# A graph-attention and mixture-of-experts layer: the node projection takes x transposed from the host, with W centred on chip

## What is computed

```python
x = x + gnn(layernorm(x), src, dst, W, b_w, a, b_a)
x = x + moe(layernorm(x), Wg, bg, W1, b1, W2, b2)

def gnn(nodes, ...):
    h = nodes @ W + b_w                      # 2500 x 512 by 512 x 512
    s_dst = h @ a[:512]; s_src = h @ a[512:]
    w = exp(leaky_relu(s_dst[dst] + s_src[src] + b_a, 0.2))
    alpha = w / segment_sum(w, dst)[dst]
    return segment_sum(alpha[:, None] * h[src], dst)
```

## Time and profile before

| | us |
|---|---|
| median of 3 runs (lowest to highest) | 864.01 (863.16 to 866.09) |
| the profiled execution, its own time | 861.91 |
| its span in the trace | 860.2 |
| busy in the span: PE, DVE, ACT, POOL | 635.0, 465.4, 370.7, 449.6 |
| mean granted TensorE clock | 0.909 of 2.4 GHz |
| first gather starts | 92.98 |

### The profile page before, as it was taken

One profiled execution on the slowest core, in us unless ns is written; L12 is line 12 of the kernel. 1 busy time (PEld: TensorE's weight loads), 2 busy tenths in 40 slices (PEclk: granted clock), 3 DMA queues, 4 the chain that ended last, 5 costly groups with the idle time before them and its releaser, 6 DMA issues.

```text
span 860.2 us, 13772 instructions
## 1 busy us (share of the span) xinstructions
PE 635.0 (74%) x2956; PEld 501.5 (58%) x2957; DVE 465.4 (54%) x1165; ACT 370.7 (43%) x982; POOL 449.6 (52%) x533
## 2 busy tenths in 40 slices
PE   4999254766776666776676676958889999999960
PEld 3777243655555555665555565745547788888840
DVE  5998433555555555565555555789495433333320
ACT  4443332434433343444343443527763454545430
POOL 5000575666666666666666666410105677777750
PEclk9999777999899998889998998887998999999995
DMA  6243475666666666666666665507994477777767
GB/s 198 100 158 106 145 214 160 180 175 177 185 175 175 178 185 175 178 182 177 177 193 169 176 192 168 146 24 263 322 376 167 90 135 136 137 132 139 134 90 249
DMA packets 58300, 146.97 MB, mean 171 GB/s; under 512 B 8868, under 2 KB 18708, under 8 KB 57880
## 3 DMA queue, kind: packets, MB, share of 16 engines
q0 software_dynamic: 35216, 106.84, 49.3%
q1 hardware_dynamic: 22968, 37.16, 12.4%
q10 hardware_dynamic: 80, 2.56, 0.9%
HBM read 118.17 MB, written 33.47 MB: 176 GB/s over the span
## 4 chain that ended last, share of the span: by engine, by line
PE 37%; DVE 22%; issue 15%; another core or an unknown queue 9%; DVEq 7%; DMA 4%; POOLq 1%; ACT 1%; POOL 1%; SPq 0%; ACTq 0%
PE ps L711 17%; PE ps L850 6%; PE ps L864 4%; DVE S L1239 4%; DVE acc L1248 4%; DVE Wt L1227 3%; PE ps L665 3%; DMA result<-y,si 2%; PE ps L840 2%; DVEq L1279 1%; PE ps L791 1%; DVEq L1248 1%; PE ps L761 1%; DMA xg<-xn_table,gi 1%
## 5 line engine op out<-in xcount | busy, mean ns | idle before, releaser
L711 PE MATMUL ps<-rows,S 128*128 128x257 f32 x1252 | 322.4, 420 | 157.6 <-DVE acc L1248 124.6
L512 POOL DMA_INDIRECT rows<-node_table,srcT x313 | 296.2, 946 | 243.4 <-issue 84.1
L711 PEld LDWEIGHTS ps<-rows,S 128*128 128x128 f32 x1252 | 260.2, 212 | 219.6 <-issue 159.2
L958 ACT ACTIVATE E<-sdst_w,rows 128x128 f32 x313 | 100.1, 390 | 281.6 <-DVE Wt L1227 150.3
L1248 DVE TENSOR_TENSOR acc<-acc,ps 64x514 f32 x160 | 110.1, 688 | 155.2 <-remote 94.5
L1239 DVE SCALAR_TENSOR_TENSOR S<-ps,lane,Wt 128x128 f32<-128x128 f32 x313 | 88.2, 345 | 22.3 <-issue 14.1
L958 ACT ACTIVATE ps<-sdst_w,rows 128x128 f32 x313 | 96.0, 351 | 0.0
L850 PE MATMUL ps<-W_e,xgT 128*128 x352 | 83.4, 380 | 0.0
L608 POOL DMA_INDIRECT result<-y,si x44 | 70.4, 1601 | 11.3 <-issue 5.8
L850 PEld LDWEIGHTS ps<-W_e,xgT 128*128 128x128 f32 x352 | 63.4, 190 | 6.9
L665 PE MATMUL ps<-Wb,xT 128*128 128x512 f32 x240 | 59.1, 403 | 2.5 <-DVE dstT L1191 1.4
(11 more groups left out here) (209 smaller groups left out, 641.9 us busy)
## 6 DMA issues: line engine op xcount, KB each, us to landing
W_e<-in_L_ffn_W_dram SPq DMA_DIRECT2D x16, 512.0 KB, 9.2
node_table<-rows SPq DMA_DIRECT2D x20, 258.0 KB, 2.6
result<-acc SPq DMA_DIRECT2D x20, 256.0 KB, 2.5
xn_table<-xn SPq DMA_DIRECT2D x20, 256.0 KB, 2.2
rows<-node_table,srcT POOLq DMA_INDIRECT x313
x_all<-in_x_dram SPq DMA_DIRECT2D x19, 256.0 KB, 3.0
out_dram<-result SPq DMA_DIRECT2D x1, 2500.0 KB, 16.7
out_dram<-result ACTq DMA_DIRECT2D x1, 2500.0 KB, 18.4
```

Of the source, the lines that this page charges most:

```text
L512: nc.gpsimd.indirect_dma_start(out=rows[:, g % RING, c, :], out_offset=None, in_=table, in_offset=bass.IndirectOffsetOnAxis(ap=srcT[:, GC ...
L711: m = pe.matmul(ps_agg[q][:, a, 0:HALF], S[:, w, c, :], rows[:, r, c, a * HALF:(a + 1) * HALF], start=(c == 0), stop=(c == n - 1))
L958: m = nc.scalar.activation(e[:, c, :], sdst_w[:, bass.ds(w, 1), :].rearrange("p w n -> p (w n)"), ACT.Exp, bias=bias, scale=scale)
```

## The change

- The host also hands over `x_cols`, x transposed in blocks: for each pair, 128 features by 4 times 256 nodes. SP loads it into `xf` (512 KB a pair) beside x itself, which is still needed for the statistics and the residual. All transposes of x on PE are gone.
- x is not normalized ahead of the product. Layernorm's mean is taken out through W: PE multiplies W by a matrix of 1/512, DVE subtracts the column means from W in place (L1124), ACT makes its high part and DVE its low part, in four pieces each. 1/std is applied behind the product, in the instruction that adds the bias (L1108).
- The high part of the transposed x is ACT's copy from SBUF (L874, both halves in one instruction). The low part is POOL's subtraction (L503), and POOL fills `acc` in ten pieces between those.
- The source and target indices come laid out by the host, and with them a copy of the targets by groups of 512, so that the smallest and largest target of a group are one reduction each.
- `load_ahead(u)` waits for the low part of pair u - 2 and its statistics. ACT's order in a step becomes `high_xT(u + 2)`, `std_of(u + 2)`, `scores(u - 1)`; DVE's `rstd_of(u)`, `normal(u + 2)`, `node_rows(u)`.

The core of the diff:

```diff
+            def load_xT(u, s):
+                sp.dma_start(xf[:, s, :, :].rearrange("p k n -> p (k n)"),
+                             x_cols[bass.ds(u, 1)].rearrange("u p c -> (u p) c")).then_inc(ld_xT[s], 16)
+            sp.dma_start(Wf[:, :, :], gnn_W.rearrange("(k p) n -> p k n", p=P)).then_inc(ld_W, 16)
+            load_xT(0, 0)
             load_x(0, 0, 0)
             load_x(0, 0, 1)
-            sp.dma_start(Wf[:, :, :], gnn_W.rearrange("(k p) n -> p k n", p=P)).then_inc(ld_W, 16)
+            load_xT(1, 1)
...
             def load_ahead(u, s, last=False):
-                for j in range(2):
-                    sp.wait_ge(xn_ok, 2 * (u - 2) + j + 1)
+                sp.wait_ge(xT_lo, u - 1)
+                load_xT(u, s)
+                sp.wait_ge(stats_ok, u - 1)
+                for j in range(2):
                     load_x(*((None, s, j) if last and j == 1 else (u, s, j)))
...
-            nc.gpsimd.memset(acc[:, :, :, :], 0.0).then_inc(ids_ok, 1)
+            for u in range(NT // 2):
+                pool.wait_ge(xT_hi, u + 1)
+                nc.gpsimd.tensor_tensor(xT[:, u % 2, 1, ...], xf[:, u % 2, ...], xT[:, u % 2, 0, ...], ALU.subtract)\
+                    .then_inc(xT_lo, 1)
+                m = nc.gpsimd.memset(acc[:, 2 * u:(2 * u + 2 if u < NT // 2 - 1 else NT + 1), :, :], 0.0)
+            m.then_inc(ids_ok, 1)
...
+            pe.wait_ge(mean_w_ok, 1)
+            pe.wait_ge(ld_W, 16)
+            for k in range(KT):
+                m = pe.matmul(ps_mean[:, :], mean_w[:, :], Wf[:, k, :], start=(k == 0), stop=(k == KT - 1))
+            m.then_inc(mean_ps, 1)
             pe.wait_ge(W_ok, 1)
             products(0, 0, True)
-            pe.wait_ge(edges_f, 1)
-            edge_columns(0)
-            edge_columns(1)
-            transposes(2, 0)
-            pe.wait_ge(edges_ok, 2)
             products(1, 1, True)
...
             def high_xT(u, s):
-                act.wait_ge(xT_ps, u + 1)
+                act.wait_ge(ld_xT[s], 16 * (u // 2) + 16 if isinstance(u, int) else u * 8 + 16 - 8 * s)
                 if not (isinstance(u, int) and u < 2):
                     act.wait_ge(h_ps, 2 * u - 2)
...
             def step(u, s, i, ahead):
-                high_xT(u + 1, 1 - s)
+                if ahead > 1:
+                    high_xT(u + 2, s)
+                    std_of(u + 2, s)
                 if not (isinstance(u, int) and u < 1):
                     scores(u - 1, 1 - s, i)
-                if ahead > 1:
-                    std_of(u + 2, s)
-                    normal(u + 2, s)
...
-                    nc.vector.tensor_tensor(halves(rows[:, s, j, 0:2 * HALF])[:, :, 0:HD], halves(ps_h[s][j]),
-                                            halves(bw_b[:, :]), ALU.add).then_inc(row_ok, 1)
+                    if j == 0:
+                        dve.wait_ge(rstd_ok, u + 1)
+                    nc.vector.scalar_tensor_tensor(out=halves(rows[:, s, j, 0:2 * HALF])[:, :, 0:HD], in0=halves(ps_h[s][j]),
+                                                   scalar=rstd[:, s, j:j + 1], in1=halves(bw_b[:, :]),
+                                                   op0=ALU.mult, op1=ALU.add).then_inc(row_ok, 1)
```

More of the change, by code:

```diff
@@ L28, in gnn_moe_kernel @@
     CH = -(-E // P)
-    CJ = -(-CH // P)
     GC = 4
@@ L637, in _ @@
             regs = [pe.alloc_register(f"pe_window{k}") for k in range(RING)]
[L638 to L646, removed]
-                for j in range(2):
-                    pe.wait_ge(xn_ok, 2 * u + j + 1)
-                    for k in range(KT):
-                        m = pe.transpose(psT[s][k // 2][:, (k % 2) * 2 * P + j * P:(k % 2) * 2 * P + (j + 1) * P],
-                                         xn[:, s, j, k * P:(k + 1) * P], ident[:, :])
-                m.then_inc(xT_ps, 1)
             def products(u, s, first):
@@ L887, in high_xT @@
             def high_xT(u, s):
-                act.wait_ge(xT_ps, u + 1)
+                act.wait_ge(ld_xT[s], 16 * (u // 2) + 16 if isinstance(u, int) else u * 8 + 16 - 8 * s)
                 if not (isinstance(u, int) and u < 2):
                     act.wait_ge(h_ps, 2 * u - 2)
-                for b in range(2):
-                    m = nc.scalar.activation(xT[:, s, 0, 2 * b:2 * b + 2, :].rearrange("p k n -> p (k n)"),
-                                             psT[s][b][:, :], ACT.Copy)
-                m.then_inc(xT_hi, 1)
-            def normal(u, s):
-                for j in range(2):
-                    act.wait_ge(rstd_ok, 4 * u + 4)
-                    if not (isinstance(u, int) and u < 2):
-                        act.wait_ge(xT_ps, u - 1)
-                    nc.scalar.activation(xn[:, s, j, :], x_of(2 * u + j), ACT.Identity, bias=shift[:, s, j:j + 1],
-                                         scale=rstd[:, s, j:j + 1]).then_inc(xn_ok, 1)
+                nc.scalar.activation(xT[:, s, 0, :, :].rearrange("p k n -> p (k n)"),
+                                     xf[:, s, :, :].rearrange("p k n -> p (k n)"), ACT.Copy).then_inc(xT_hi, 1)
+            high_xT(0, 0)
             std_of(0, 0)
-            normal(0, 0)
-            act.wait_ge(ld_W, 16)
-            nc.scalar.activation(Wb[:, 0, :, :], Wf[:, :, :], ACT.Copy).then_inc(W_hi, 1)
+            for k in range(KT):
+                act.wait_ge(Wc_ok, k + 1)
+                nc.scalar.activation(Wb[:, 0, k, :], Wf[:, k, :], ACT.Copy).then_inc(W_hi, 1)
+            high_xT(1, 1)
             std_of(1, 1)
-            normal(1, 1)
-            high_xT(0, 0)
             def scores(u, s, i):
@@ L1565 @@
     arrays, args = {}, []
+    laid = {name: _np.asarray(a) for name, a in inputs.items()}
+    n, d = laid["x"].shape
+    edges = laid["src"].shape[0]
+    x_rows = _np.zeros((-(-n // 256) * 256, d), laid["x"].dtype)
+    x_rows[0:n] = laid["x"]
+    laid["x_cols"] = x_rows.reshape(-1, 256, d // 128, 128).transpose(0, 3, 2, 1).reshape(-1, 128, 2 * d)
+    groups = -(-edges // 512)
+    src_p, dst_p = _np.zeros(groups * 512, _np.int32), _np.full(groups * 512, 4095, _np.float32)
+    src_p[0:edges], dst_p[0:edges] = laid["src"], laid["dst"]
+    laid["src"], laid["dst"], laid["dst_groups"] = (
+        src_p.reshape(-1, 128).T, dst_p.reshape(-1, 128).T, dst_p.reshape(-1, 512))
     for name in _INS:
-        a = _np.ascontiguousarray(inputs[name])
+        a = _np.ascontiguousarray(laid[name])
         if a.ndim == 0:
```

120 lines of the change are left out of this document (43 added, 77 removed).

## The result

The changed kernel takes **877.54 us** (median of four runs, 873.45 to 881.40) against 863.59 for the kernel before on the same chip (861.05 to 866.09): a ratio of **1.0163**, with a 95% interval of 1.0129 to 1.0198. It is 14 us slower. The forecast was 869.5, and its range ended at 877.5. The first gather was forecast at about 98 us.

The account below looks back on a forecast made before the run. DVE was taken as the bound, PE close behind. Scores at 33.0, six periods of 8.3 us less 0.3, then DVE's last rows gave 93.7 against 88.16: +5.5 us, so 864.0 becomes 869.5, range 861.4 to 877.5.

Parts of the forecast that it names:

- The sign: The whole kernel: the change makes it slower, chance 0.71.
- mechanism: First stage: DVE stands still 2.7 us of each step, waiting for the transfer of x.
- The circle: First stage: scores, stores, loads, statistics, root and scores wait in turn, 8.3 us a step against 6.98; chance 0.60.
- The start: Before the first products: W, the mean's products and W's low parts; products start at 17.7 instead of 16.16.
- The loads' term of the circle: Link from the first load issue to x landed, 1 MB a pair: 4.8 us, bounds 4.1 to 5.5.
- Scores to first load: Link from ACT's scores through SP's two stores to the first load of x: 1.65 us.
- The second tile's statistics to the scores' end: Link of DVE's second-tile statistics, ACT's square root, two score instructions and hops: 1.85 us.
- The tail: Stage's end on DVE: rows of pairs 7, 8 and 9, 3.9 us each, with two reciprocals of 0.2.
- POOL's subtraction, costed at nothing: POOL's low part of the transposed x: no cost, covered by over 6 us available in each step.
- Rival 3: First stage: the circle does not close and PE's pace holds, 9.5 us less, 854.5; chance 0.13.
- Rival 4: First stage: POOL and DVE hinder each other; dots take twice as long, 7.5 us more, 871.5; chance 0.13.

Follow-up runs that it names:

- after_again: The changed kernel again, unedited, for a second trace and more times: 807.68 us, ratio 1.0198 to the kernel before.
- scores_first: Changed kernel with ACT's scores(u - 1) put back ahead of high_xT(u + 2) and std_of(u + 2): 795.86 us, ratio 1.0046 to the kernel before.
- loads_first: Changed kernel with SP's loads of a pair ahead of the stores of the pair four before: 789.79 us, ratio 0.9980 to the kernel before.
- both_first: Changed kernel with both order edits, ACT's scores first and SP's loads first: 795.63 us, ratio 1.0043 to the kernel before.
- loads_rows: Changed kernel with SP's loads first and DVE's row instructions of both tiles ahead of their dots: 856.01 us, ratio 0.9899 to the kernel before.
- loads_rows_again: The kernel of loads_rows measured again with more rounds: 858.26 us against 865.05 for the kernel before, ratio 0.9913.
- both_fill: Kernel of both_first with POOL filling zeros in place of the subtraction, leaving out x's low part: 851.72 us, ratio 0.9844 to the kernel before.
- loads_rows_wait: Kernel of loads_rows with POOL's subtraction for pair 1 waiting for W's low parts: 856.12 us against 865.05 for the kernel before, ratio 0.9890.
- both_pieces: Kernel of both_first with POOL's subtraction cut into four of 256 columns: 861.15 us, ratio 0.9962 to the kernel before.
- before_scores_last: Kernel before with only ACT's scores(u - 1) moved behind std_of(u + 2) and normal(u + 2): 879.19 us against 862.64, ratio 1.0199.

## Why the prediction was right or wrong

The sign and the mechanism held. DVE was to wait 2 to 3 us for x in each step, and waits 2.9 to 3.2. The circle was to be the cause: two different cuts open it, and planted in the kernel before it closes there. **The size failed**: +5.5 us forecast, 11.5 in the profiled execution and 14.0 in the medians. In the forecast's own steps:

- **The start** was right in the profiled execution. W was there at 6.71 (forecast 7.1), the mean's products took 5.46 (5.3), the products started at 17.15 (17.7), and pair 0's scores were done at 33.16 (33.0).
- **The loads' term of the circle is the step that failed.** Scores to first load was 1.65 and is 1.78 in the turn shown. The second tile's statistics to the scores' end was 1.85 and is 1.68 (49.71 to 51.39). The loads were put at 4.8 and measure 5.65 (44.06 to 49.71), above the upper bound of 5.5. The transfer itself is hardly to blame: from the first issue to the first tile's statistics it is 4.99 us. What was forgotten is the 0.66 us of those statistics. I let the second tile's start wait for the last transfer alone, as if the first tile's x came well before. But the issues of the two tiles are 0.57 us apart, and DVE, once it has waited for the first, goes on to the second without a wait: both tiles are there within some half a microsecond, so the first tile's statistics stand behind the landing, in series. The three terms make 9.11 in the turn shown and 9.09 in the mean, not 8.3, and over the six steps (33.44 to 87.97) 54.5 us, not 49.5: **+5.0 us**. The 0.3 us that the last tile, half a tile, was to save are in it: they did not come, as that tile's x kept DVE another 0.81 us (the row at 86.26).
- **The tail** was 1.0 us short, counted from the stores of pair 6 to the last dot. The rows of a pair take 4.32 us (95.48 to 99.80), not 3.9 plus 0.2, in part because the instruction with the scaling takes 0.74 and not 0.69; that is 0.6 us over three pairs. The other 0.4 is that DVE begins these rows 0.8 us ahead of the stores of pair 6, and the sum had it 1.2 ahead.
- Start 0.2, circle 5.0, tail 1.0: together 6.2 us, and the profiled execution exceeds its forecast of 867.4 by 6.1.
- **POOL's subtraction, costed at nothing**, is the second error. The rule of the Trainium skill cited ahead of the result (GPSIMD Engine Reference, sections 1 and 8) is borne out: DVE instructions with two operands in SBUF and GpSimd do contend. In these runs GpSimd's subtraction did so, and its fills did not. The duration that the prediction took from section 3.1 of the same page of the Trainium skill, 2.25 us as an estimate, was near too: 2.35 us where POOL met nothing and 2.45 in the mean. But the prediction took this as a matter of POOL's length and of DVE's steady pace, and there the circle left idle time enough (the mean dot is 780 ns, and most of the excess over 690 is in one dot). The collision that can count is at the start, where W's low part is on the path: 4.66 us or 2.49. Of the seven traces in which POOL's whole subtraction may meet it, six (after_again, scores_first, loads_first, both_first, loads_rows and loads_rows_again) have the long form of 4.66; the first trace of the changed kernel has the short one, and is also the fastest of its four runs, 4.1 us below their median where 2.1 was assumed. That the other three runs had the long form, and that it makes up the other 2 us of the median, is likely and not shown: they left no trace, and in after_again only 1.2 us of the later start reached the first stores.
- **Rival 3**, the open circle at PE's pace, was priced at 854.5, 9.5 us less than before. With the circle open, the kernel gives 12.5 us less without the subtraction (both_fill) and 8.9 with few collisions left (loads_rows_wait). So the price was near for a kernel that was not the one changed. Its pace was not quite right: PE's products were put at 5.71 us a step and need 5.44, and DVE's 5.69 is the longer (both_fill).
- **Rival 4** asked for dots that lose over 2.7 us a step. They lose 1.5 once the circle is open, and it then decides the time: 7.18 against 5.69 us a step. So it was not a rival to the circle; the circle hid it.
- The granted clock fell to 0.92 in the stage, from 1.00, once PE had gaps between its products. It did not enter the sum, and none of the circle's links in the chain shown is PE's.

## What to carry to other kernels

When a change reorders an engine's program, walk from each wait through the queue behind it until you come back or reach the start; a circle that holds a DMA has its whole landing time in each turn, here over 4 of 9.1 us, while every engine had idle time. In such a circle count what an engine does serially after the landing, for all pieces that land together, and not the last piece alone. And before giving DVE's work to POOL, look at what DVE does in that time: beside the row instructions (one operand in PSUM) and the statistics (a single operand) it was free here, beside dots with two operands in SBUF it cost more than it saved (1.49 us against 1.22 in both_first).

## What was not expected of the hardware

- A dot of DVE (two operands in SBUF) that starts while POOL subtracts (two operands in SBUF) ends some 0.55 us after POOL does: 28.89 and 28.34, 50.95 and 50.41. A dot alone takes 0.69 us, so it looks less like sharing than like waiting for the other's instruction to end, and both_pieces bears that out. It holds the other way as well: POOL's subtraction took 2.96 us where it met a running piece of DVE's, 2.34 to 2.41 where it met none. Statistics, row instructions (one operand in PSUM) and POOL's fills took part in none of this.
- POOL took 0.74 us for 256 columns (median) and 2.35 for 1024. With its waits for dots, cutting the subtraction up cost 12 us more of POOL's time over the stage.
- Cutting one circle twice can be worse than once: both_first is 5.8 us slower than loads_first. By the traces it keeps the two engines at the phase in which they collide.
- The same kernel before took 791.6 us beside the first four runs and 862 to 865 beside all others. The record gives chip 1 for the runs at 791.6 and also for those at 862.64 beside before_scores_last, so that this is a difference between chips is not shown; its cause is open.
